# Class maximum over all keys taken off the keys; correction and mask products left out for late queries, GpSimd zeroes instead

## What is computed

```python
x = L0_attn_x                                   # (4, 1024, 256)
h = _layernorm(x) * (1 + ca) + sa
x = x + ga * attention(h)
h = _layernorm(x) * (1 + cb) + sb
x = x + gb * experts(h)                         # 8 experts, each takes 512 rows
# attention: 16 heads of 16 features, 1024 positions
q, k, v = (keep_largest_abs(proj(w), 1) for w in (wq, wk, wv))
scores = where(causal, q @ k.T / 4, -inf)
attn = softmax(keep_top(scores, 64))            # the others become -inf
out = (attn @ v) @ wo.T
```

## Time and profile before

| | us |
|---|---|
| median of 3 runs | 1103.88 |
| lowest, highest | 1103.40, 1104.36 |
| the profiled execution | 1100.29 |
| its span in the profile | 1098.6 |
| TensorE busy | 951.7 |
| VectorE busy | 654.0 |
| ScalarE busy | 509.0 |
| GpSimd busy | 189.3 |

### The profile page before, as it was taken

One profiled execution on the slowest core, in us unless ns is written; L12 is line 12 of the kernel. 1 busy time (PEld: TensorE's weight loads), 2 busy tenths in 40 slices (PEclk: granted clock), 3 DMA queues, 4 the chain that ended last, 5 costly groups with the idle time before them and its releaser, 6 DMA issues. The chain is left out here.

```text
span 1098.6 us, 19097 instructions
## 1 busy us (share of the span) xinstructions
PE 951.7 (87%) x7528; PEld 524.2 (48%) x7528; DVE 654.0 (60%) x1393; ACT 509.0 (46%) x691; POOL 189.3 (17%) x280
## 2 busy tenths in 40 slices
PE   6769999999999998999989999986214999999996
PEld 5533444345444444534435545435103666666664
DVE  6766668567677666585683674625486555444441
ACT  3655767773767756476775464661000122221110
POOL 3410222000222000031200000000003433344222
PEclk9879999999999989999998998997555999999998
DMA  4000000000100011100002012001551144442111
GB/s 154 1 1 21 1 21 1 1 1 2 58 20 1 1 42 37 59 1 1 1 1 79 1 40 79 1 1 50 185 210 41 41 113 103 112 111 43 21 20 20
DMA packets 34861, 46.69 MB, mean 42 GB/s; under 512 B 2184, under 2 KB 30928, under 8 KB 34640
## 3 DMA queue, kind: packets, MB, share of 16 engines
q1 hardware_dynamic: 28624, 36.89, 9.9%
q0 software_dynamic: 6144, 8.52, 4.8%
HBM read 32.69 MB, written 12.72 MB: 41 GB/s over the span
## 5 line engine op out<-in xcount | busy, mean ns | idle before, releaser
L899 ACT ACTIVATE p_buf<-ps 128x1024 f32<-128x1024 f32 x288 | 279.2, 1023 | 181.6 <-PE ps L424 115.9
L415 PE MATMUL ps<-qx,kd 32*128 32x512 f32 (+3 forms) x1280 | 149.4, 535 | 23.5 <-DVE p_buf L1234 19.0
L2044 ACT ACTIVATE h_t<-ps,b_t 128x512 f32<-128x512 f32 x64 | 44.0, 687 | 244.6 <-PE ps L1984 244.6
L446 PE MATMUL ps<-p_buf,vv 128*17 128x512 f32 (+3 forms) x1664 | 155.6, 475 | 0.0
L1234 DVE SCALAR_TENSOR_TENSOR p_buf<-ps,p_buf 128x1024 f32<-128x1024 f32 x64 | 76.1, 1219 | 75.8 <-ACT p_buf L899 70.1
L1984 PE MATMUL ps<-tok_t,w_sb 128*128 128x512 f32 x256 | 114.4, 606 | 0.0
L1994 PE MATMUL ps<-w_sb,h_t 128*128 128x256 f32 x512 | 112.5, 380 | 0.8 <-ACT h_t L2044 0.8
L1994 PEld LDWEIGHTS ps<-w_sb,h_t 128*128 128x128 f32 x512 | 96.6, 190 | 15.3 <-ACT h_t L2044 1.6
L415 PEld LDWEIGHTS ps<-qx,kd 32*128 32x128 f32 x1280 | 53.5, 191 | 63.7 <-issue 47.6
L357 PE MATMUL ps<-w_t,h_t 128*128 128x512 f32 (+1 forms) x224 | 78.9, 496 | 0.6 <-ACT w_t L833 0.4
L1984 PEld LDWEIGHTS ps<-tok_t,w_sb 128*128 128x128 f32 x256 | 49.2, 194 | 59.3 <-issue 59.1
(11 more groups left out here) (285 smaller groups left out, 1435.7 us busy)
## 6 DMA issues: line engine op xcount, KB each, us to landing
w_sb<-in_L_ffn_w_dram SPq DMA_DIRECT2D x16, 1024.0 KB, 9.5
h_table<-xr SPq DMA_DIRECT2D x3, 1056.0 KB, 4.6
x_in<-in_L_attn_x_dram SPq DMA_DIRECT2D x6, 512.0 KB, 3.7
out_dram<-xr SPq DMA_DIRECT2D x3, 1024.0 KB, 5.1
xr<-in_L_attn_x_dram SPq DMA_DIRECT2D x3, 1024.0 KB, 5.5
h_table<-xr SPq DMA_DIRECT2D x2, 528.0 KB, 3.0
xr<-in_L_attn_x_dram SPq DMA_DIRECT2D x2, 512.0 KB, 5.1
p_buf<-in_L_wmod_dram SPq DMA_DIRECT2D x1, 1024.0 KB, 8.6
```

Source lines behind the costliest of these rows:

```text
L415: pe.matmul(o, key, qx[r, par, t0:t0 + w], start=True, stop=False)
L446: m = pe.matmul(ps[32 * h:32 * h + HD + 1, 6, o:o + w], vv[:, (gi // NG) % 2, i, HG * (gi % NG) + h, :], p_of(gi, u)[:, h, lo:lo + w], sta ...
L899: act.activation(p_of(gi, u)[:, 2 * a:2 * a + 2, :], buf(w), ACT.Exp, scale=0.25).then_inc(free_of(w)[0], 1)
L2044: act.activation(h1_t[:, f, :], ps[:, L1_BANKS[f % 3], :], ACT.Relu, bias=b1_t[:, e * FO + f:e * FO + f + 1]).then_inc(s_h1, 1)
```

## The change

The keys of a class have their maximum over all 1024 positions (`k_max`) taken off, in `kd` and in `ks` (key block 0). Then a score is never above zero for any query, late keys included. For queries of the second half (from 512 on, "late pieces") the correction product L419 is left out. For the first half it stays, with `qm = (mx - k_max) * qx` and `over` at -(1 - 2^-7): it puts the running maximum back in place of the class maximum. The scan `mx` is over 512 columns only.

The mask product L424 is left out in late pieces too. Instead GpSimd sets to zero, in the exponentials of units 2, 3 and 8, the entries of later keys (`tri`, four `affine_select`s of 128 x 4 x 128 per pass), and the value products of those units wait for it on a new semaphore `f_tri`. GpSimd's queue is written out by pass instead of by batch. In the opening all scores wait for both halves, and `one_feature(0, 7)` comes before `first_half_keys`, `negatives(0)` after `second_half_queries`.

The core of the diff:

```diff
-        mx = sf("mx", [P, T], BF16)
-        qm = sf("qm", [P, 2, T], BF16)
+        mx = sf("mx", [P, 512])
+        qm = sf("qm", [P, 2, 512], BF16)
+        k_far = sf("k_far", [P, T], BF16)
+        k_max = sf("k_max", [P, 1])
+        k_max1 = sf("k_max1", [P, 1])
...
                     if u == 0:
-                        pe.wait_ge(f_kp, gi + 1 if gi == 0 else gi + 2)
-                        pe.wait_ge(f_uq, gi + 1 if gi == 0 else gi + 2)
+                        pe.wait_ge(f_kp, gi + 2)
+                        pe.wait_ge(f_uq, gi + 2)
...
-                        diag = t0 == P * i
+                        early = t0 < 512
+                        diag = early and t0 == P * i
                         last = (i, t0, w) == UNITS[u][-1]
                         for h in range(HG):
...
-                            pe.matmul(o, key, qx[r, par, t0:t0 + w], start=True, stop=False)
-                        for h in range(HG):
+                            m = pe.matmul(o, key, qx[r, par, t0:t0 + w], start=True, stop=not early)
+                            if h % 2 and last and not early:
+                                m.then_inc(full_of(("S", gi, u, h // 2))[0], 1)
+                        for h in range(HG * early):
...
                 def pv(gi, u):
                     c = 0 if u < 3 else 1
+                    if u in (3, 8):
+                        pe.wait_ge(f_tri, tri_of(gi, u))
...
                 def pv_late(gi):
+                    pe.wait_ge(f_tri, tri_of(gi, 2))
...
+                def tri(gi, u):
+                    for a in range(2):
+                        pool.wait_ge(*free_of(("S", gi, u, a)))
+                    lo = 0
+                    for i, t0, w in UNITS[u]:
+                        if t0 == P * i and t0 >= 512:
+                            p = p_of(gi, u)[:, :, lo:lo + P]
+                            m = pool.affine_select(p, p, [[0, HG], [1, P]], ALU.is_ge, 0.0, base=0, channel_multiplier=-1)
+                        lo += w
+                    m.then_inc(f_tri, 1)
...
+                for gi in range(GA):
+                    b, g = divmod(gi, NG)
+                    pre, post = b + 1 < B, b > 0
+                    tiles = pre and g in (1, 2)
+                    t0 = 4 * (g - 1)
+
+                    if g == 1 and post:
+                        second_rstd(b - 1, (0, 1))
+                    if g == 0 and pre:
                         first_rstd(b + 1, 0)
...
+                    if tiles:
+                        keep(b + 1, t0)
+                    tri(gi, 2)
+                    tri(gi, 3)
+                    if tiles:
+                        keep(b + 1, t0 + 1)
+                    if g == 1 and pre:
                         first_rstd(b + 1, 1)
...
+                    if tiles:
+                        keep(b + 1, t0 + 2)
+                        keep(b + 1, t0 + 3)
+                    tri(gi, 8)
...
                 def keys(n):
                     par = n % 2
                     kx = kd[:, par, :]
-                    dve.tensor_tensor_scan(mx[:, :], kx, kx, 0.0, ALU.max, ALU.max)
+
+                    dve.tensor_tensor_scan(mx[:, :], kx[:, 0:512], kx[:, 0:512], 0.0, ALU.max, ALU.max)
+                    dve.tensor_reduce(k_max1[:, :], kx[:, 512:T], AX.X, ALU.max)
+                    dve.tensor_scalar(k_far[:, :], k_not[:, :], -FAR, None, ALU.mult)
...
                     dve.drain()
-                    dve.scalar_tensor_tensor(kx, k_not[:, :], -FAR, kx, ALU.mult, ALU.add).then_inc(f_kp, 1)
+                    dve.tensor_tensor(k_max[:, :], mx[:, 511:512], k_max1[:, :], ALU.max)
+                    dve.drain()
+                    dve.tensor_scalar(ks[:, par, :], ks[:, par, :], k_max[:, :], None, ALU.subtract)
+                    dve.scalar_tensor_tensor(kx, kx, k_max[:, :], k_far[:, :], ALU.subtract, ALU.add).then_inc(f_kp, 1)
...
-                    dve.tensor_tensor(qm[:, par, :], qx[:, par, :], mx[:, :], ALU.mult)
+                    dve.scalar_tensor_tensor(qm[:, par, :], mx[:, :], k_max[:, :], qx[:, par, 0:512], ALU.subtract, ALU.mult)
...
-                for t in range(2, 7):
+                for t in range(2, NT):
                     one_feature(0, t)
                 first_half_keys()
-                one_feature(0, 7)
                 first_half_queries()
                 zero_rank(0)
                 losers(0)
-                negatives(0)
                 second_half_keys()
                 second_half_queries()
+                negatives(0)
```

More of the change, by code:

```diff
@@ L197, in build_kernel @@
         FAR = 2.0 ** 60
-        f_const, f_ones = sem("f_const"), sem("f_ones")
+        f_const, f_ones, f_tri = sem("f_const"), sem("f_ones"), sem("f_tri")
         f_x, f_xr, f_xfree = (sem(n) for n in ("f_x", "f_xr", "f_xfree"))
@@ L225, in build_kernel, with tri_of @@
         ring_at, m_at, pv_at = {}, {}, {}
+        DIAG = (2, 3, 8)
+        def tri_of(gi, u):
+            return len(DIAG) * gi + DIAG.index(u) + 1
         def buf(u):
@@ L454, in pv @@
                             pe.wait_ge(*free_of(("Z", gi, c, a)))
-                        else:
+                        elif u not in (3, 8):
                             pe.wait_ge(*free_of(("S", gi, u, a)))
@@ L773, in _ @@
                 pool.memset(late[:, :], 0.0)
-                pool.memset(over[:, :], -(1.0 + 2.0 ** -7))
+                pool.memset(over[:, :], -(1.0 - 2.0 ** -7))
                 pool.memset(upto[:, :], 1.0)
@@ L1080, in first_half_keys @@
                     dve.drain().then_inc(f_cnr, 1)
-                    dve.tensor_tensor_scan(mx[:, h], kd[:, 0, h], kd[:, 0, h], 0.0, ALU.max, ALU.max)
+                    dve.tensor_tensor_scan(mx[:, :], kd[:, 0, h], kd[:, 0, h], 0.0, ALU.max, ALU.max)
+                    dve.tensor_scalar(k_far[:, h], k_not[:, h], -FAR, None, ALU.mult)
                     dve.scalar_tensor_tensor(kb[:, :], k_not[:, 0:P], FAR, kd[:, 0, 0:P], ALU.mult, ALU.add)
@@ L1106, in second_half_keys @@
                     dve.drain()
-                    dve.tensor_copy(carry[:, :], mx[:, 511:512])
-                    dve.drain()
-                    dve.tensor_tensor_scan(mx[:, h], kd[:, 0, h], kd[:, 0, h], carry[:, :], ALU.max, ALU.max)
+                    dve.tensor_reduce(k_max1[:, :], kd[:, 0, h], AX.X, ALU.max)
+                    dve.tensor_scalar(k_far[:, h], k_not[:, h], -FAR, None, ALU.mult)
                     dve.tensor_tensor(n_lo[:, :], n_lo[:, :], left[:, T - 1:T], ALU.min)
                     dve.drain()
-                    dve.scalar_tensor_tensor(kd[:, 0, h], k_not[:, h], -FAR, kd[:, 0, h], ALU.mult, ALU.add).then_inc(f_kp, 1)
+                    dve.tensor_tensor(k_max[:, :], mx[:, 511:512], k_max1[:, :], ALU.max)
+                    dve.drain()
+                    dve.tensor_scalar(ks[:, 0, :], ks[:, 0, :], k_max[:, :], None, ALU.subtract)
+                    dve.scalar_tensor_tensor(kd[:, 0, :], kd[:, 0, :], k_max[:, :], k_far[:, :], ALU.subtract, ALU.add).then_inc(f_kp, 1)
+                    dve.scalar_tensor_tensor(qm[:, 0, :], mx[:, :], k_max[:, :], qx[:, 0, 0:512], ALU.subtract, ALU.mult)
                 def second_half_queries():
```

18 lines of the change are left out of this document (3 added, 15 removed).

## The result

| | before | changed |
|---|---|---|
| median, us | 1104.12 | 1087.65 |
| lowest, highest | 1103.40, 1106.68 | 1086.06, 1088.35 |
| ratio, 95% interval | | 0.9845 (0.9825 to 0.9864) |
| span of the profiled execution | 1098.6 | 1086.5 |

The change saves 16.5 us, 1.5%. The forecast was 28 us less, at 1076, with a range of 1057 to 1092: faster as foretold, inside the range, and by a good half of what was expected.

A forecast was written before the change was run, and what follows sets the result against it. TensorE was taken to bound on average, but VectorE from unit 3's turn back in pass 3. Savings of 33.0 us, less 1.2 for the opening and 4 for the clock, gave 27.8 and 1076 us, range 1057 to 1092.

The forecast's parts named there:

- VectorE sets the pace from the turn back in unit 3 onward: Pass 3, also pass 1: VectorE, not TensorE, sets the pace there, so later TensorE savings pass only in part.
- rival 1: Attention passes: TensorE bounds throughout, so 48.6 less 1.2 us is saved, giving 1056; chance 0.2 for 1064 or less.
- 48.6 us of TensorE time: Late pieces, 16 passes: removed correction (2.1 us) and mask products (1.0) free 3.1 us of TensorE per pass.
- rival 3: Score groups: the scores' own end takes the removed products' whole place, time stays at 1104; chance 0.03 within 0.2%.
- Four first passes of a batch: they pass whole: Units 5 to 8 in the four first passes of a batch: their 1.76 us reaches the end whole, 7.0 us.
- The clock, 4 us: TensorE's granted clock: two to three more falls to 1.2 GHz at 1.7 us each, cost 4 us, ends 0 and 10.
- The collision: Unit 3's select against VectorE's scan in SBUF: scan taken first, at no cost; otherwise 16 x 0.6 = 9.6 us.
- rival 2: Unit 3: select gets in ahead of the scan each time, costing 9.6 us, giving 1086, up to 1092; chance 0.15.
- GpSimd's selects: Units 2, 3 and 8: 64 selects, four per pass, some 0.58 us each, covered and costed at nothing.
- Rival 4: GpSimd is late: selects of 8 us make value products wait, 1128 us, slower; chance 0.04.
- VectorE's exchange, near zero: VectorE per pass: 1.8 us saved on scan and qm, 1.5 added for maximum, k_far and small operations; net near zero.
- The opening, 1.2 us: Program start: scores wait for both halves of keys and queries, cost 1.2 us, ends 0.6 and 3.3.

The follow-up runs named there:

- f1: The changed kernel, unaltered, run again on another chip beside the kernel before: 1087.71 us, ratio 0.9840.
- f4: Changed kernel with six fillers ahead of unit 5, six in the opening, and unit 3's select held behind the scan: 1079.81 us, ratio 0.9766 to the kernel before.
- e1: Kernel before with only the late correction and mask products left out, output not the reference's: 1080.33 us for 1100.6, ratio 0.9819.
- e2: Changed kernel without GpSimd's 64 selects and the value products' waits on them, output not the reference's: 1080.51 us, ratio 0.9808 to the kernel before.
- e4: Changed kernel with GpSimd's select of unit 3 held until the key_counts scan is done: 1083.57 us, ratio 0.9819 to the kernel before.
- f3: Changed kernel with VectorE's k_not (and a drain) done twice in each of 15 key_counts: 1104.44 us, ratio 1.0000 to the kernel before.
- e3: Changed kernel with six 512-column filler products on TensorE in the wait ahead of unit 5's scores: 1079.36 us, ratio 0.9802 to the kernel before.
- f2: Kernel before with the change's opening alone (waits of unit 0, new places of one_feature(0, 7) and negatives(0)): 1104.47 us, ratio 0.9994.

## Why the prediction was right in sign and short in size

The start of `lost(n)` on TensorE divides the trace into passes. From one to the next, in us:

| pass | before | changed | changed again (f1) | f4 | saving forecast (part by part, without clock) |
|---|---|---|---|---|---|
| 1 | 44.9 | 44.2 | 44.0 | 44.0 | 1.4 |
| 2 | 43.5 | 42.1 | 42.1 | 42.7 | 1.6 |
| 3 | 34.4 | 34.5 | 35.8 | 32.6 | 2.1 |
| 4 | 45.9 | 45.6 | 44.1 | 44.2 | 2.7 |
| 7 | 41.2 | 42.8 | 43.5 | 42.4 | 2.1 |
| 8 | 50.1 | 46.6 | 47.5 | 45.7 | 2.7 |
| 14 | 35.5 | 33.5 | 33.9 | 32.4 | 2.1 |
| 1 to 14 | 603.4 | 588.9 | 590.4 | 581.0 | 27.2 |

Two traces of the same kernel differ by up to 1.6 us in a pass, in pass 4 by whether the clock fell, so a single row is not to be read to its tenth. Pass 7 became longer in all three: in the kernel before the clock fell only at its end, at 402 us, in the others up to 24 us earlier. What comes behind pass 14, to the end of the program, did not get shorter (390.7 us before, 392.9 and 390.0 changed, 395.1 in f4).

A second cut is steadier: on TensorE, from the start of the turn back behind unit 3's scores to the start of unit 5's scores, in us. VectorE's `key_counts` and masks lie in it, and unit 4's correction products (0.21 us).

| passes | before | e1 | e2 | e4 | changed | f3 |
|---|---|---|---|---|---|---|
| 1, 2, 5, 6, 9, 10 | 8.59 | 8.64 | 8.64 | 8.64 | 8.64 | 9.14 (pass 2: 9.35) |
| 3, 7, 11, 13, 14 | 6.01 | 6.06 | 6.06 | 6.06 | 6.48 | 7.25 |
| 4, 8 | 8.60 | 8.65 | 8.72, 8.65 | 8.99 | 8.99, 8.91 | 9.67 |
| 12 | 7.38 | 7.43 | 7.43 | 7.43 | 7.69 | 8.47 |

- *VectorE sets the pace from the turn back in unit 3 onward: right in pass 3 and its like, too wide elsewhere.* This was the reading against TensorE's 87% busy share and against rival 1 (1056). The second table shows it: unit 4's products are gone in e1, and the stretch did not get shorter (6.01 to 6.06). f3 adds to it directly. But in the six passes with tiles it is VectorE's wait for an eviction, behind TensorE's projection, that decides up to the masks. Only behind the masks does VectorE run without a gap there; in pass 1, L1263 (old L1220 of the earlier trace rows) still begins with none:

```profile
147.73 1.12 DVE L1263 SCALAR_TENSOR_TENSOR lw<-ps,y_mx,tie 128x128 bf16<-128x128 f32 x4
```

- *48.6 us of TensorE time: too large.* The step took start-to-start times of L419 as the price of its removal. The scores' own end took back 0.1 to 0.2 us per group, which rival 3 had named as a whole or nothing. Units 2 and 3 save 0.34 and 0.36 (0.40 and 0.56 were put down), units 4 to 7 0.21 or 0.22 each; unit 8 gained more than put down (from the first scores to the next product 2.07 before, 1.08 after). That is some 2.5 us a pass and 40 in all. The forecast's own sum with these sizes gives an estimate of 28 us instead of 33.0, most of the loss in units 2 and 3, which everything waits for. Of the 33.0 e1 left 20.3, clock losses included.
- *"Four first passes of a batch: they pass whole": not shown, and wrong in pass 4.* Its wait ahead of unit 5 grew from 2.54 to 3.09 us. In the changed kernel's first trace the clock fell behind it and the pass saved 0.3 us; in f1's it did not fall, and the pass saved 1.8 of the 2.7 (first trace, then f1):

```profile
247.98 1.14 PE L424 MATMUL ps<-qx,kd 32*128 32x512 f32 x8 [3.09 <-DVE p_buf L1277]
```

```profile
249.92 1.14 PE L424 MATMUL ps<-qx,kd 32*128 32x512 f32 x8 [3.09 <-DVE p_buf L1277]
```

  Pass 8 saved 3.5 and 2.6 us in the two traces, pass 12 1.9 and 0.3.

- *The clock, 4 us: right in kind, too small.* The deficit grew by 15.6 us, not by two or three falls of 1.7; e3 buys some 4.4 us of time back with fillers in one place, and in f4 the deficit is 21.6. TensorE's busy time fell by 27 us and not by the 45 to 60 foretold; the low clock, at which its products are longer, is a part of that.
- *The collision: rival 2's condition held, and the forecast's choice, the scan first, was wrong.* The select came first in 14 of 15 passes, mostly by 0.07 us; the rows ahead had the two at 209.3 and 209.36, too near to tell. It cost 2.5 to 3.7 us in the medians, not 9.6. Each scan lost 0.36 us on average and not 0.6, and there are 15 scans, not 16. And the second table shows in which passes that reached TensorE: 0.42 us in five, about 0.3 in three, nothing in the six with tiles, 2.9 us in all. So it is luck that rival 2's number, 1086, lies next to the measured 1087.65: most of the missing 11 us has other causes. The Trainium skill's page "SBUF — State Buffer", section "Who interferes with whom", has the rule right: the scan (two SBUF inputs) is stretched, the mask (one from PSUM) in e4 is not.
- *GpSimd's selects: right.* 0.63 us against 0.58, and no value product waited for one. Rival 4, the slower one, had no footing.
- *VectorE's exchange, near zero: right.* L1229 and L1230 took 0.66 and 0.42 against 0.6 and 0.4 (rows at 213.05 and 213.63 above). A wait that the sum did not have: ahead of `zero_rank` TensorE stands for VectorE's L1285, up to 1.5 us a time and 6.5 in all, where it was 2.2 before; in f1 it was 1.9. That a later `kd` causes it is not shown.
- *The opening, 1.2 us: right at the first score, short behind it.* (The terms given, 2.6 less 0 to 2, make 0.6 to 2.6, not 3.3.) Alone it costs 0.7 us in f2's trace and nothing in its median. In the changed kernel's trace the clock was low from 70 to 75 us, which the forecast had not put there, and pass 0's own saving was gone at its end.

Of the missing 11 us, then, some 5 are the price of the removals and some 3 the collision, both estimates from the rows above; the remaining 3 or so would be the clock beyond its 4 us and waits such as that at `zero_rank`. What stays open is how these last divide: 2 to 5 us is near what these intervals can separate.

## What to carry to other kernels

Removing work from the busiest engine is worth what the next queue in each stage leaves of it; look for stretches in which another engine runs without a gap between two of its handovers, and price the change by what precedes them. The first instruction to make shorter is then there, not on the engine with the highest busy share (e4, which takes 0.42 us out of such a stretch, points that way; no run here shortened it by more). If waits grow on TensorE, its granted clock can fall, and filler products in the wait can be cheaper than the fall. They cost where the wait is shorter than they are: in e3 0.62 us in each of six passes. Fillers only where TensorE stands longer than they take were not run.

## What the runs showed of the hardware that was not expected

- TensorE stood 1.61 us in pass 3, and its granted clock fell from 2.4 to 1.2 GHz behind that wait (0.68 in the stage 210 to 215 us). With six bfloat16 products of 512 columns in that place (1.47 us) it stayed at 2.4 GHz. The length of the last wait alone does not decide: it fell behind one of 0.72 us (pass 1, 0.67 in 130 to 135 us) and not behind one of 3.09 (pass 4 of f1, 1.00 in 245 to 255 us).
- At 2.4 GHz, four row groups of 512-column float32 scores need 1.07 to 1.16 us from start to start when a product over all 128 rows follows, and 0.93 to 0.96 when a bfloat16 product of the same row groups does.
- Of a scan of VectorE and a select of GpSimd, the one that starts second is stretched: the scan from 2.29 to 2.71 us when the select was 0.07 us ahead, the select from 0.63 to 2.53 when the scan was 0.19 ahead (pass 0).
- A tensor_scalar of VectorE with one operand (k_not, 0.68 us alone) took 1.12 us beside a select of GpSimd in f3. Two inputs in SBUF are not needed for a collision. The same section of the Trainium skill allows for it: it counts tensor_scalar among the operations that can take the shared ports in a two-port mode, and the trace agrees.
